# Two graph layers on one core: attention's one-hots turned two tiles at a time, register loads in three parts, edge features turned in groups

## What is computed

```python
# layer 0: attention with 4 heads, over each target's edges
h = (h @ W.T).reshape(N, H, OUT)
alpha = leaky_relu(a_src[src] + a_dst[dst], 0.2)
ex = exp(alpha - segment_max(alpha, dst)[dst])
out = segment_sum(h[src] * (ex / segment_sum(ex, dst)[dst]), dst) + bias
# layer 1: an MLP on every edge, summed by row (= src)
msg = concatenate([x[row], x[col], edge_attr], axis=-1)
h = relu(msg @ W1 + b1)
out = segment_sum(h @ W2 + b2, row)
```

## Time and profile before

| | |
|---|---|
| median of 3 runs | 5811.69 us (5804.1 to 5815.06) |
| profiled execution, its own time | 5807.29 us |
| its span | 5805.4 us |
| busy PE / DVE / ACT / POOL | 5114.6 / 4028.8 / 2891.4 / 3923.5 us |
| mean granted TensorE clock | 0.938 of full speed |
| indirect DMAs, gathers / scatters | 1591.7 / 1587.3 us for 1612 each |

### The profile page before, as it was taken

The page is one execution under the profiler, slowest core; times in us unless marked ns, Lnnn a source line. Parts: engine busy times, 40 slices in busy tenths (PEclk is TensorE's granted clock), DMA queues, the critical chain, the costliest instruction groups (busy, mean ns, idle before and its releaser), DMA issues.

```text
span 5805.4 us, 160391 instructions
## 1 busy us (share of the span) xinstructions
PE 5114.6 (88%) x34498; PEld 4012.9 (69%) x34499; DVE 4028.8 (69%) x14406; ACT 2891.4 (50%) x8241; POOL 3923.5 (68%) x3713
## 2 busy tenths in 40 slices
PE   4888888888888886899999999999987999999999
PEld 3677777776677775667666666666665777777777
DVE  6777777777777778555555555555555888888887
ACT  3555555555555553333333333333224777777776
POOL 4777777777777775677777777777776545555553
PEclk6898888888888887999999999999998999999999
DMA  4422222222222225899888899988896999999997
GB/s 108 161 54 52 52 53 53 52 53 53 53 52 52 53 62 165 261 262 269 261 263 260 255 262 260 257 261 253 256 256 182 214 214 211 213 216 215 213 214 187
DMA packets 860289, 993.31 MB, mean 171 GB/s; under 512 B 307992, under 2 KB 663224, under 8 KB 859774
## 3 DMA queue, kind: packets, MB, share of 16 engines
q1 hardware_dynamic: 662494, 608.23, 40.1%
q0 software_dynamic: 190592, 378.22, 24.3%
q10 hardware_dynamic: 6816, 3.38, 0.2%
HBM read 726.65 MB, written 262.76 MB: 170 GB/s over the span
## 4 chain that ended last, share of the span: by engine, by line
PE 55%; DMA 12%; DVE 10%; issue 10%; POOL 7%; DVEq 4%; ACT 2%; POOLq 0%; SPq 0%; ACTq 0%
PE bank L1525 12%; PE bank L1684 11%; PE bank L1617 7%; DMA xr<-arena 7%; PE bank L1619 7%; POOL xr L542 7%; PE bank L1674 6%; DMA arena<-p_tab,arena 3%; PE bank L1453 3%; DVE arena L1042 2%; DVEq L246 2%; DVE arena L935 2%; PE bank L1607 1%; DMA arena<-h_tab,arena 1%; PE bank L1665 1%
## 5 line engine op out<-in xcount | busy, mean ns | idle before, releaser
L494 POOL DMA_INDIRECT arena<-h_tab,arena x1612 | 1591.7, 987 | 582.9 <-issue 399.5
L542 POOL DMA_INDIRECT xr<-arena x1612 | 1587.3, 985 | 510.7 <-issue 350.3
L1525 PE MATMUL bank<-arena 128*128 128x136 f32 x6448 | 1299.7, 329 | 96.6 <-DVE arena L1042 8.1
L703 ACT ACTIVATE arena<-bank 128x256 f32<-128x256 f32 x1612 | 595.9, 385 | 1405.6 <-PE bank L1619 1050.2
L556 POOL DMA_INDIRECT arena<-p_tab,arena x428 | 668.4, 1562 | 658.7 <-DMA arena<-p_tab,arena 443.4
L1525 PEld LDWEIGHTS bank<-arena 128*128 128x128 f32 x6448 | 966.3, 211 | 201.8 <-issue 109.0
L621 ACT ACTIVATE arena<-bank 128x256 bf16<-128x256 bf16 x1612 | 618.2, 384 | 888.9 <-PE bank L1453 833.6
L1617 PE MATMUL bank<-arena 128*128 128x256 f32 x3224 | 1010.3, 395 | 42.4 <-DVE arena L1236 25.2
L1619 PE MATMUL bank<-arena 128*128 128x256 f32 x3224 | 972.5, 383 | 28.6 <-DVE arena L1252 25.5
L1684 PE MATMUL bank<-arena 128*128 128x257 f32 x3424 | 898.8, 385 | 3.8 <-ACT arena L780 3.2
L1042 DVE TENSOR_TENSOR arena<-arena,bank 128x272 f32 x1612 | 692.2, 429 | 181.5 <-PE bank L1525 163.7
(11 more groups left out here) (253 smaller groups left out, 6596.8 us busy)
## 6 DMA issues: line engine op xcount, KB each, us to landing
arena<-xr SPq DMA_DIRECT2D x428, 516.0 KB, 3.9
arena<-q_tab SPq DMA_DIRECT2D x1612, 128.0 KB
arena<-in_edge_attr SPq DMA_DIRECT2D x61, 832.0 KB
arena<-rel_tab SPq DMA_DIRECT2D x124, 224.0 KB
arena<-h_tab,arena POOLq DMA_INDIRECT x1612
xr<-arena POOLq DMA_INDIRECT x1612
arena<-rel_tab SPq DMA_DIRECT2D x124, 192.0 KB
xr<-arena SPq DMA_DIRECT2D x26, 516.0 KB
```

The source lines that it names most:

```text
L494: pool.indirect_dma_start(G[:, q, t, :], None, h_tab, bass.IndirectOffsetOnAxis(ap=idx[:, q, t:t + 1], axis=0)).then_inc(sem(f"gath{q}"), 16)
L542: pool.indirect_dma_start(xr, bass.IndirectOffsetOnAxis(ap=pos[:, q, t:t + 1], axis=0), Rb[:, t, :], None).then_inc(sem(f"scat{m}"), 16)
L1525: last = pe.matmul(PSB[3 + t % 2][:, k * H * MW:(k + 1) * H * MW], OH[:, (t + 2 * q) % 4, k * P:(k + 1) * P], flat(msg[:, t, :, :]), start ...
```

## The change

In attention a transposition takes two tiles: `turn` waits for two one-hots and transposes them into one bank, ACT copies 512 columns in one instruction, and `ohT` holds two pairs. The expansions follow two tiles behind, the last two of a batch in the next batch. DVE makes one-hots two tiles ahead, those of the next batch's first two tiles at the end of a batch. `bins` reads 8, 9 and 9 registers, on DVE at tiles 0, 8 and 17, on PE at tiles 1, 9 and 18 (and 2 for the late expansions at the start). DVE's second half of the logits' sums moves from tile 1 to tile 3.

In the target stage edge features are turned and copied out in groups of two pairs (EG), 7 groups a batch (NEG), on banks 4 and 6 in turn. The first group of the next batch is turned at tile 22. One-hots have 13 buffers (RO) and are made 5 tiles ahead (HOTS). All ranks use bank 5; counts, ranks and what follows them stand one to four tiles later or earlier. For batch 0, ranks 1 and 2 are issued on PE behind node(0). `t49` and `EAT` lie in other memory.

```diff
+RO = 13
+HOTS = 5
+EG = 2
+NEG = -(-(BT // 2) // EG)
...
+        LOADS = [(k * BT // 3, (k + 1) * BT // 3) for k in range(3)]
+        egroup = lambda j: range(j * EG, min((j + 1) * EG, BT // 2))
...
-        def bins(engine, b, count):
+        def bins(engine, b, lo, count):
...
-            def turn_out(b, t, first=False):
-
-                act.wait_ge(sem("ohT_ps"), b * BT + t + 1)
-                if not (first and t < 2):
-                    act.wait_ge(sem("expanded"), b * BT + t - 1)
-                A.activation(ohT[:, t % 2, :], PSB[t % 2][:].bitcast(BF16)[:, 0:2 * P], ACT.Copy).then_inc(sem("ohT_ready"), 1)
+            def turn_out(b, s, g, first=False):
+
+                act.wait_ge(sem("ohT_ps"), b * NG2 + g + 1)
+                if not (first and g < 2):
+                    act.wait_ge(sem("expanded"), b * BT + 2 * g - 2)
+                k = (s * NG2 + g) % 2
+                A.activation(flat(ohT[:, k, :, :]), PSB[k][:].bitcast(BF16)[:, 0:4 * P], ACT.Copy).then_inc(sem("ohT_ready"), 1)
...
             def batch(i, q, ahead3=True, ahead2=True, ahead1=True, table=""):
                 b, n = 2 * i + q, 2 * i + q + 1
-                regs = bins(ENG.DVE, b, BT)
+                regs = []
                 for t in range(BT):
-                    if ahead2:
-                        hot(b + 2, q, t)
+                    if ahead2 and t + 2 < BT:
+                        hot(b + 2, q, t + 2)
+                    for lo, hi in LOADS:
+                        if t == lo:
+                            regs += bins(ENG.DVE, b, lo, hi - lo)
...
-                        if ahead1:
-                            logits(b + 1, 1 - q, 1)
                     if t >= 2:
                         add_up(b, t - 2, regs)
+                    if ahead1 and t == 3:
+                        logits(b + 1, 1 - q, 1)
...
-                add_up(b, BT - 2, regs)
-                add_up(b, BT - 1, regs)
+                for t in range(2):
+                    if ahead3:
+                        hot(b + 3, 1 - q, t)
+                    add_up(b, BT - 2 + t, regs)
...
-                    V.tensor_scalar(OHT[:, (t + 2 * q) % 4, :], DB[:, t * P:(t + 1) * P], pcol, None,
+                    V.tensor_scalar(OHT[:, t % RO, :], DB[:, t * P:(t + 1) * P], pcol, None,
...
+                    V.tensor_copy(EAT[:, u % 2, 0:n, :], PSB[(4, 6)[u % 2]][:, 0:n * P].rearrange("p (k e) -> p k e", e=P)).then_inc(sem("ea_out"), 1)
+                for t in range(HOTS):
+                    hot(t)
...
-                        if t in (11, 14, 18):
-                            rank(r, {11: 0, 14: 1, 18: 2}[t])
+                        if t in (13, 17, 20):
+                            rank(r, {13: 0, 17: 1, 20: 2}[t])
...
-                    for m in range(2):
+                    for m in range(3):
                         rank(0, m)
                         own(0, 0, m)
...
+            def turn(b, s, g, first=False):
+                u = (s * NG2 + g) % 2
+                pe.wait_ge(sem("oh_ready"), b * BT + 2 * g + 2)
...
             def batch(b, q, ahead2=True, ahead1=True, first=False, table=""):
-                if ahead2:
-                    regs = bins(ENG.PE, b + 2, BT)
+                regs, late = [], bins(ENG.PE, b + 1, BT - 2, 2) if ahead1 else []
...
                 for t in range(BT):
+                    if ahead2 and t % 2 == 0:
+                        turn(b + 2, q, t // 2)
+                    if t < 2 and ahead1:
+                        expand(b + 1, 1 - q, BT - 2 + t, late[t])
                     if ahead2:
-                        turn(b + 2, q, t)
-                        if t:
-                            expand(b + 2, t - 1, regs)
+                        for lo, hi in LOADS:
+                            if t == lo + 1:
+                                regs += bins(ENG.PE, b + 2, lo, hi - lo)
+                        if t >= 2:
+                            expand(b + 2, q, t - 2, regs[t - 2])
...
-                o = PSB[5 + m % 2]
+                o = PSB[5]
...
+                def turn_ea(c, p, j):
+                    u = p * NEG + j
+                    if not (first and c is b and j < 2):
+                        pe.wait_ge(sem("ea_out"), c * NEG + j - 1)
+                    for k in egroup(j):
+                        done = pe.transpose(PSB[(4, 6)[u % 2]][:, (k - j * EG) * P:(k - j * EG + 1) * P], flat(EAb[:, p, 2 * k:2 * k + 2, :]), ident)
+                    done.then_inc(sem("eaT_ps"), 1)
...
+                        if t == 22:
+                            ea_there(r, s, last)
+                            turn_ea(r, s, 0)
...
             counts(0, 0, 0, BT)
             rank(0, 0, 0)
-            rank(0, 0, 1)
             for c in range(NCH):
                 node(c)
                 if c == 0:
+                    rank(0, 0, 1)
                     rank(0, 0, 2)
```

More of the change, by code:

```diff
@@ L652, in _ @@
             act.wait_ge(sem("cols_used"), 2)
-            for t in range(BT):
-                turn_out(0, t, True)
+            for g in range(NG2):
+                turn_out(0, 0, g, True)
             act.wait_ge(sem("rb_init"), 2)
@@ L659, in _ @@
             chain_exp(0, True)
-            for t in range(BT):
-                turn_out(1, t)
+            for g in range(NG2):
+                turn_out(1, 1, g)
             def batch(b, q, ahead2=True, ahead1=True, first=False):
@@ L703, in targets @@
                     A.activation(Rb[:, t, 0:HID], PSB[(t + 2 * q) % 4][:, 0:HID], ACT.Copy).then_inc(sem("r_out"), 1)
-                    if ahead and t == 9:
+                    if ahead and t == 8:
                         counts_out(b + 1)
@@ L707, in targets @@
                         A.activation(hcol.unsqueeze(1), h2T[:, bass.ds(part, 1), :], ACT.Copy).then_inc(sem("part_in"), 1)
-                    if part is not None and t == 22:
+                    if part is not None and t == 24:
                         act.wait_ge(sem("pq_ps"), NCH * NQ + part + 1)
@@ L1144, in _ @@
             logits(1, 1, 0)
+            for t in range(2):
+                hot(2, 0, t)
             batch(0, 0)
@@ L1292, in _ @@
                 if c == 1:
-                    rank(0, 2)
-                    own(0, 0, 2)
                     total(0)
@@ L1462, in expand @@
                 for k in range(2):
-                    last = pe.matmul(ab_ps[half][:, j, :, :].rearrange("p s c -> p (s c)"), ohT[:, t % 2, k * P:(k + 1) * P],
-                                     flat(aT3[:, bass.ds(regs[t] + k, 1), :, :]), start=(k == 0), stop=(k == 1))
+                    last = pe.matmul(ab_ps[half][:, j, :, :].rearrange("p s c -> p (s c)"), ohT[:, (s * NG2 + g) % 2, t % 2, k * P:(k + 1) * P],
+                                     flat(aT3[:, bass.ds(reg + k, 1), :, :]), start=(k == 0), stop=(k == 1))
                 last.then_inc(sem("expanded"), 1)
@@ L1489, in _ @@
             pe.wait_ge(sem("hx_used"), NCH)
-            regs = bins(ENG.PE, 0, BT)
-            for t in range(BT):
-                turn(0, 0, t, True)
-                if t:
-                    expand(0, t - 1, regs, True)
-            expand(0, BT - 1, regs, True)
+            regs = bins(ENG.PE, 0, 0, BT)
+            for g in range(NG2):
+                turn(0, 0, g, True)
+                for t in range(max(2 * g - 2, 0), 2 * g):
+                    expand(0, 0, t, regs[t], True)
+            for t in range(BT - 2, BT):
+                expand(0, 0, t, regs[t], True)
             chain_resets(0)
@@ L1657, in _ @@
                     targets(2 * i + q, q, parts=NT - 1)
-            targets(NB - 2, 0, part=NT - 1)
+            targets(NB - 2, 0, last=True, part=NT - 1)
             targets(NB - 1, 1, final=True)
```

143 lines of the change are left out of this document (70 added, 73 removed).

## The result

The changed kernel takes **6932.7 us** (median of four runs, 6923.1 to 6944.7); the kernel before took 5810.4 in the same comparison. The ratio is 1.193, 95% interval [1.191, 1.196]. The prediction was 5790 us, range 5752 to 5820, with 12 in 100 for slower. It had the wrong sign and missed by 1143 us.

A forecast was written before the change was run, and what follows sets the result against it. POOL was taken to bound attention and targets. Attention -24 us, its end and targets 0, node stage +3.5 made -20.5; with -1 for the first batches' fewer waits, the forecast was 5790 us, range 5752 to 5820.

The forecast's parts named there:

- POOL bounds both stages: Attention and targets: POOL's gathers and scatters set the time, the target stage completely, attention but for 49 us.
- 49.3 us: Attention: POOL's real waits at the gathers, beyond the first wait and fixed gaps; 24 us of them were to go.
- the fixed gap: POOL's queue: 0.3046 us idle ahead of each gather or scatter, which the diff doesn't touch.
- the one-hots two ahead: Attention: tiles 0 and 1 made while DVE waits for PE, taking 2 x 0.2 us off the batch's start.
- with mains 22 to 25 queued behind it: Targets: the next batch's first edge-feature turn at t = 22 makes PE wait for a load, delaying these; priced at 0 us.
- nine of the loads, 0.7 us each: Attention: loads at t = 8 on DVE and t = 9 on PE add 1.4 us before the tenth gather's aggregate.
- Rival D: Attention: a register load costs 0.195 us, so the kernel slows, +74 us to 5886; range 5823 to 5886, chance 0.12.
- The clock comes back sooner: Attention, after a batch's start: PE regains full clock earlier; a tile's aggregate takes 0.72 us there for 1.27.
- Fewer, larger turns: Attention: 13 turns of 512 columns for 26 of 256 save ACT 10.0 to 8.1 us a batch, worth nothing.
- The node stage, +3.5: Node stage: DVE waits for rank 1 on PE, partly repaid by faster products; net +3.5 us, bounds 0 and +9.
- nothing in the diff touches them: Targets: scatters stay at 0.985 us on average whatever PE does, so the stage changes by 0 us.
- the cover: Targets: 5.7 us a batch in which ACT waits for scatters, hiding changes on the other engines.

The follow-up runs named there:

- e1: The changed kernel with attention's one-hot of tile t + 2 made behind the add of tile t - 2, not ahead of it: 6226.2 us, ratio 1.070.
- e3: The changed kernel with attention's one-hots made one tile ahead, not two, still in front of the add: 6166.8 us.
- e2: The kernel before with only attention's one-hots made two tiles ahead, in front of the add: 6314.1 us.
- e11: The kernel before with only its register read cut into 8, 9 and 9 registers: 6106.3 us, ratio 1.050.
- e4: The changed kernel with four unused matmuls a tile added on PE in attention: 6606.9 us.
- e9: The changed kernel with attention's one-hots behind the add and the 26 registers read at once: 6024.1 us, ratio 1.037.
- e14: The changed kernel with attention's one-hots one tile ahead, in front of the add, and one register read, on a slow chip: 6962.9 us, ratio 0.959.
- e15: e9's kernel with the target stage's one-hots held to at most seven tiles ahead, on a slow chip: 7012.5 us, ratio 0.964.
- e16: e14's kernel with the target stage's one-hots held to at most seven tiles ahead, on a slow chip: 6970.1 us, ratio 0.960.
- e12: e9's kernel with the target stage's bins_of moved from tile 0 to tile 4: 6027.8 us, ratio 1.036.
- e5: The same kernel as e9, on a chip where the kernel before took 7378 us: 7088.5 us, ratio 0.960.

## Why the prediction was wrong

**That POOL bounds both stages** was right for the kernel before, and so was the count of 49.3 us that it could win. The rest of the sum asked only how much of 49 us comes back, and took for granted that nobody else could become later by more. Of the 1685.9 us idle at L502, 1152 are waits beyond the first and the fixed gap, where 25 were forecast.

**The step that failed first: "the one-hots two ahead".** The prediction priced the moved one-hots as 2 x 0.2 us taken off the batch's start. It never followed the wait inside `hot` to its end. In the target stage it did name what is queued behind a new wait ("with mains 22 to 25 queued behind it"), and not here. The wait's text didn't change; its index did, from t to t + 2, and with four wide buffers the thing waited for moved from an aggregate two adds old to the very one whose add is queued behind. The runs show what stands in its place: a ring through PE, ACT and DVE, worth 703 us of attention by the order (e1), 769 by the distance (e3), and 499 alone in the kernel before (e2).

**The term that was mis-sized: "nine of the loads, 0.7 us each".** 2.00 / 26 = 0.077 us was taken as the price of one register. The mean over a read of 26 from an aligned start says nothing of nine from word 17: 2.08 us, 0.231 us each. The second read, the only one for which the sum had a wait, was near: 0.7 us forecast, 0.86 measured. The third, at t = 17, was put at 0.7 us as well and at no wait at all, and it takes 2.08 us on DVE and 2.18 on PE. Rival D, "a load costs 0.195 us", had the right direction, with 12 in 100, but it put its price on the second read and came to +74 us; the runs show +291 for the split alone (e11), with that price in the third. So D's sign is in part luck. The page that stood behind D (the Trainium skill, Runtime: NRT & Kernel Launch, section Instruction fetch mechanics) has about 200 ns for each register. The trace comes near it only for the read from word 17 (0.231); for the one read of 26 it is 0.080.

**"The clock comes back sooner"** failed with the first step. It went from 0.88 to 0.56 in attention instead, and that made the loss at least 323 us larger (e4). The prediction had both levels in the earlier trace rows, 1.27 and 0.72 us for one tile's aggregate, and used them only as a gain.

**"Fewer, larger turns"** were put at nothing, and the runs leave that open. e9, with the order and one read put right, is still 151 us longer in attention than before. One-hots two ahead for one account for 66, if what e3 has over e1 holds here too. The other 85 no run takes apart: the turns of two tiles, the two late expansions with their own read of two registers on PE (0.55 us a batch), and the later sum of the logits are all in it. Where PE, DVE and ACT bound, these parts together won time (e14).

**The node stage, +3.5**: from the last aggregate to the first scatter it is 103.0 us for 99.1, +3.9. The mechanism was as forecast too: DVE waits for rank 1, and its products, now with POOL idle beside them, take 0.67 and 0.47 us for 1.71 and 1.73.

```profile
3351.03 0.67 DVE L1218 TENSOR_TENSOR arena<-bank,arena 128x490 f32<-128x490 f32 x1 [6.82 <-PE bank L1610]
3351.73 0.67 DVE L1224 TENSOR_TENSOR arena<-arena 128x490 f32<-128x490 f32 x1
...
3352.84 0.47 DVE L1224 TENSOR_TENSOR arena<-arena 128x294 f32<-128x294 f32 x1
```

**Targets, "nothing in the diff touches them"**: the fixed gap before a scatter stayed (510.7 and 511.7 us), the stage isn't held by PE or DVE, and the cover was there: all as said. But the scatters themselves are 34 ns longer, 55 us in all, in every kernel that has the new target stage (1018 to 1024 ns on the first chips, 1003 to 1015 on the others) and in none that doesn't (983 to 986). The diff doesn't touch POOL's queue, but it changes what DVE does beside it. The long scatters lie beside DVE's unbroken stretches. POOL and DVE of the kernel after, two timelines:

```profile
4504.13 1.02 POOL L550 DMA_INDIRECT xr<-arena  x1 [0.30 <-issue]
4505.45 2.28 POOL L550 DMA_INDIRECT xr<-arena  x1 [0.30 <-issue]
```

```profile
4504.02 1.26 DVE L1252 TENSOR_SCALAR arena<-arena 128x128 f32<-128x128 bf16 x6 [0.22 <-issue]
4505.20 1.68 DVE L1207 TENSOR_TENSOR arena<-arena 128x294 bf16<-128x294 bf16 x4
4506.80 0.23 DVE L1213 TENSOR_SCALAR arena<-arena 128x26 f32 x1
4506.95 0.28 DVE L1252 TENSOR_SCALAR arena<-arena 128x128 f32<-128x128 bf16 x1
```

With 13 buffers DVE makes six one-hots in a row and goes straight on with `bins_of` (the four L1207), and the scatter that starts beside them ends 0.85 us after them. In the kernel before DVE stands still just ahead of the same four, and the scatter beside them takes 1.14 us:

```profile
2544.79 0.29 DVE L1252 COPY arena<-bank 128x128 f32<-128x128 f32 x1 [0.69 <-PE bank L1607]
...
2545.19 1.69 DVE L1191 TENSOR_TENSOR arena<-arena 128x294 bf16<-128x294 bf16 x4
```

```profile
2546.17 1.14 POOL L542 DMA_INDIRECT xr<-arena  x1 [0.30 <-issue]
```

A scatter's median is 0.971 us in both kernels. What all scatters take above it is 77 us after and 22 before. Of this, 42 and 12 us belong to scatters beside the four products. The Trainium skill (SBUF — State Buffer, section Who interferes with whom) says that a DVE instruction with two SBUF inputs contends with a GpSimd one that reads SBUF. The long scatter beside the four L1207 agrees. But the kernel before has the same four instructions (its L1191), and the scatters beside them exceed 0.971 by 0.10 us in the mean, for 0.38 after. So the rule names the partner and not the reason for the difference.

The traces point at the stretch that DVE works without a gap (none over 0.06 us) just ahead of the four. Its median is 0.40 us before and 1.51 after. Scatters that start beside the products behind a stretch under 0.7 us take 1.12 us in the mean before (59 of them); behind a longer one they take 1.56 after (55), and in the kernel before, too, the two such take 2.39. The experiments didn't test this. Pacing left the stretch at 1.25 us in the median (e15, e16), and the few scatters behind a short one took 1.17 and 1.14 us (3 and 4 of them). Moving `bins_of` made the stretch longer, 2.79 us (e12), though there nine scatters behind a short one took 1.41. No run cut the stretches off, and none tried the other suspects, the copies of 256 columns and the other memory of `t49` and `EAT`. The cause of the 55 us stays open.

## What to carry to other kernels

When a diff makes an operation earlier, write down what its wait asks for with the new index, follow that through each ring of buffers until an engine is met, and look whether something that engine needs is queued behind the waiting instruction. A ring of four and a step of two was enough here for 12% of the kernel's time (703 us of 5810). Don't price a part of a long instruction by its mean: find where it starts, or keep the whole. And look at the granted clock when a chain makes PE wait: here it fell with it, and the wait was paid twice.

## What the runs showed of the hardware

A register read's time goes by where it begins: read to DVE's registers, 26 from word 0 took 2.07 us, 8 from word 0 or 8 0.60, 9 from word 8 0.85, 10 from word 16 1.07, and 9 from word 17 2.08 (2.18 on PE). Words are counted in a batch's row, and every second row begins four words past a multiple of eight, so it isn't a boundary of eight that counts. Word 17 is the only odd start; whether evenness or a multiple of four counts, no run separates. Nor do the numbers give a price for each register: the later stage's read of 12 registers, from a multiple of eight words in its own row, takes as long as 9 from word 8.

```profile
L260 DVEq TENSOR_LOAD <-arena x108: 845/851/1282, 5562.7 to 6880.5; - x108
```

Filling PE's idle time with unused matmuls made a kernel 4.7% faster (6933 to 6607 us), with the granted clock in attention at 0.88 for 0.56.

The same kernel took 5810, 5815, 5816, 7265, 7276 and 7378 us in six comparisons. In the profiles from the slow ones (of other kernels; the kernel before has none there) POOL, DVE and ACT have the same durations, the granted clock in attention is lower, and waits end without a releaser in the trace. An order of merit found on one chip doesn't hold on the other: e5's kernel is 4.0% faster than before on one and 3.7% slower (as e9) on the other.
